# The causal mask moved from GpSimd to TensorE in a one-core attention + mixture-of-experts block, with its neighbours reordered

## The chip, the core and the metric

One NeuronCore of a Trainium2 chip runs the whole block as one program. The metric is the device time of that program in microseconds (us), the median of the runs shown. Lower is better. The five engines run side by side: TensorE (PE, with its weight loads as PEld), VectorE (DVE), ScalarE (ACT), GpSimd (POOL) and SyncE (SP, which here only issues transfers). They meet through semaphores: each engine works its own list in order and stops at a wait until the count is reached.

## What is computed

```python
x = L0_attn_x                                   # 4 sequences x 256 tokens x 512
xn = _layernorm(x)
# attention: 32 heads of 16, 8 key/value groups of 4 heads
scores = jnp.einsum('bhqd,bhkd->bhqk', q, k)
scores = jnp.where(causal, -jnp.inf, scores)    # key later than query
weights = softmax(scores * HD**-0.5)
att = (weights @ v) @ Wo + bo
# experts: 16, the 4 best of each token, plus one shared expert
z = silu(x @ Wg.T) * (x @ Wu.T)
ffn = sum_over_chosen(cw * (z @ Wd.T)) + shared
out = x + att + ffn
```

## The kernel before

The 1024 tokens are normalised first. An opening stretch (to about 124 us of the span) projects queries and keys, splits them into bf16 parts and stores them in HBM, runs the shared expert over eight tiles of 128 tokens (n = 0 to 7), and builds the routing tables. It writes x plus the shared expert's result to `out` in HBM.

Then comes the main stretch: **47 slots** of 128 routed token rows. In one, TensorE transposes the gathered rows of the next slot (`rows_transpose`, L1219), multiplies by the slot's expert in two halves (`gate_up_half` 0 and 1, L1178), transposes the gated result of the slot before (`z_transpose`, L1186), and does the down product of two slots back (`down`, L1168). The slot's expert may be a new one: then SP has loaded its weights (`load`, L364, one of two buffers) and told ACT so (`announce`, L360, a wait for the landing and then a count); ACT makes their high part (L635), DVE the low part of the gate and up weights (`gu_low`, L994) and POOL the low part of the down weights (`down_low`, L500). TensorE's `gate_up_half` 0 waits for DVE's.

Attention is threaded through the slots. Each of the four sequences b has twelve slots j and eight groups g of four heads; the table `BESIDE = ((0, 1), (2,), (3,), (4, 5), (6,), (7, 8), (9,), (10, 11))` says which slots lie beside which group. In a group's first slot TensorE makes the transposed scores of the group (`scores`, L1285 and L1287, keys on partitions, into banks 0 to 2), ACT takes their exponential (`numerators`, L707; the tile is `pexp`, which lies in `xn` and is called xn in the rows), and TensorE then puts other scores into the same three banks, from which DVE finds the maxima of the group four ahead (`scores_for_max`, L1198 and L1203; `maxima`, L979). The two calls share the banks, so each waits for the other's reader. The `numerators` are split into two fp16 parts, `phi` by ACT (`high16`, L713) and `plo` by DVE (`low16`, L1036), which TensorE multiplies with the values in the next group (`weighted`, L1301). Between `numerators` and `high16`, POOL sets to zero the entries whose key is later than the query (`causal`, L484, two selects per group).

The maxima of four groups are collected (`negm_split`), transposed by TensorE (`maxima_transpose`, L1210), copied by ACT and sent by ACT's queue into two extra rows of the query tile (`minus_maxima`, L666 and L668, semaphore `nm_in`). `scores` of groups 0 and 4 waits for that transfer.

POOL's list in a slot is: the group's selects, the gather of the slot three ahead (`gather`, L475), the indirect add of a finished slot into `out` (`add_rows`, L495, 256 KB, tile `ysb`), then `down_low`. All adds into `out` are strictly one after the other, since rows may repeat. Attention's result of a sequence (tile `att`, called xn in the rows) is added in one transfer of 512 KB (`add_attention`, L517), beside the next sequence's j = 4. ACT writes the `ysb` tile of a slot only when the add of two slots before has landed.

## Time and profile before

| | |
|---|---|
| median of 3 runs | 553.87 us (553.21 to 555.04) |
| the profiled execution | 553.7 us |
| its span in the trace | 552.0 us |
| mean granted TensorE clock | 0.945 |
| PE busy | 453.3 us |
| DVE busy | 357.0 us |
| ACT busy | 284.3 us |
| POOL busy | 274.6 us |

Busy time is the union of an engine's instructions over the span. The span leaves 1.7 us of the profiled execution outside. A timeline row gives start and length in us, counted from the span's start, and in brackets the idle time of that engine before the row and what ended it. The granted clock is the share of 2.4 GHz that TensorE had: 1.00 is 2.4 GHz and 0.50 is 1.2 GHz.

### The profile page before, as it was taken

What the parts mean: (1) busy time and instruction counts of PE and PEld (TensorE: products, weight loads), DVE (VectorE), ACT (ScalarE), POOL (GpSimd) and SP (SyncE); (2) the same over time, 40 slices, a digit from 0 to 9 for tenths busy, and PEclk for the clock granted to TensorE, in tenths of its full rate; (3) what the DMA queues carried; (4) which work ended last, traced back from release to release, by engine and by line L of the source; (5) the groups of instructions that cost most, each with busy time, mean ns of one, the idle gap of its engine ahead of it and who ended that gap; (6) DMA issues with size and microseconds to landing.
All of it is one profiled execution on the core that took longest, in us unless ns stands there. A gap on an engine that the chain in (4) does not pass through costs nothing.

```text
span 552.0 us, 9709 instructions
## 1 busy us (share of the span) xinstructions
PE 453.3 (82%) x2960; PEld 338.6 (61%) x2960; DVE 357.0 (65%) x604; ACT 284.3 (52%) x434; POOL 274.6 (50%) x235
## 2 busy tenths in 40 slices
PE   0998969968398899889987789987779999998870
PEld 0967748845276676557755567565556776766640
DVE  6488743776177678857779797578367655955620
ACT  2532222615266567745676577377276545756610
POOL 2111609632244575565467687263467534654630
PEclk9999979998699899999988899999979999998996
DMA  7915952549634644895588775856655433254233
GB/s 273 356 29 132 256 204 68 145 134 172 257 96 80 172 73 95 240 241 130 92 202 238 203 202 111 211 103 182 153 135 83 77 72 54 63 95 80 39 48 48
DMA packets 31813, 77.91 MB, mean 141 GB/s; under 512 B 3984, under 2 KB 11664, under 8 KB 28848
## 3 DMA queue, kind: packets, MB, share of 16 engines
q1 hardware_dynamic: 18864, 45.92, 27.1%
q0 software_dynamic: 11792, 27.27, 26.4%
q10 hardware_dynamic: 1104, 4.06, 3.5%
q8 instruction: 27, 0.44, 0.3%
q14 instruction: 26, 0.21, 0.1%
HBM read 54.04 MB, written 23.07 MB: 140 GB/s over the span
## 4 chain that ended last, share of the span: by engine, by line
PE 37%; DMA 24%; DVE 13%; ACT 8%; issue 8%; POOL 3%; SPq 2%; ACTq 1%; DVEq 1%; POOLq 0%
PE psum L1178 10%; DMA out<-ysb,tab 9%; PE psum L1168 8%; DMA wraw<-wexp 5%; DMA q_parts<-stage 3%; PE psum L1198 3%; PE psum L1313 3%; DVE wsplit L994 3%; ACT xn L707 3%; DMA out<-xn 3%; DVE plo L1036 3%; PE psum L1131 2%; ACT wsplit L635 2%; PE psum L1203 2%; PE psum L1115 2%
## 5 line engine op out<-in xcount | busy, mean ns | idle before, releaser
L1178 PE MATMUL psum<-wsplit,xgT 128*128 x564 | 163.2, 428 | 14.6 <-DVE wsplit L994 14.5
L495 POOL DMA_INDIRECT out<-ysb,tab x47 | 81.8, 1740 | 127.8 <-ACT ysb L660 87.0
L1178 PEld LDWEIGHTS psum<-wsplit,xgT 128*128 128x128 f32 x564 | 105.3, 200 | 35.2 <-issue 17.4
L1168 PE MATMUL psum<-wsplit,zT 128*128 (+1 forms) x330 | 87.7, 401 | 9.6 <-issue 4.6
L1036 DVE TENSOR_TENSOR plo<-xn,phi 128x1536 f16<-128x1536 f32 x32 | 63.4, 1980 | 36.7 <-ACT phi L713 35.2
L1168 PEld LDWEIGHTS psum<-wsplit,zT 128*128 128x128 f32 x330 | 61.0, 188 | 25.8 <-issue 13.4
L989 DVE TENSOR_TENSOR xgT<-psum,xgT 128x512 fp32r<-128x512 f32 x47 | 32.3, 687 | 53.5 <-ACT xgT L631 53.2
L475 POOL DMA_INDIRECT xg<-xn_rows,tab x47 | 57.1, 1215 | 17.3 <-PE psum L1219 8.8
L979 DVE TENSOR_REDUCE negm<-psum 128x4 f32<-128x512 f32 x64 | 58.6, 949 | 7.4 <-PE psum L1203 7.4
L484 POOL TENSOR_SCALAR_AFFINE_SELECT xn<-xn 128x512 f32<-128x512 f32 x64 | 53.3, 961 | 20.2 <-ACT xn L707 20.2
L635 ACT ACTIVATE wsplit<-wraw (+1 forms) x48 | 48.8, 1048 | 15.5 <-SPq L360 9.7
L707 ACT ACTIVATE xn<-psum 128x1536 f32<-128x1536 f32 x32 | 46.3, 1446 | 19.5 <-PE psum L1287 12.4
L500 POOL TENSOR_TENSOR wsplit<-wraw,wsplit (+1 forms) x16 | 45.4, 2838 | 20.6 <-ACT wsplit L635 20.4
L660 ACT ACTIVATE ysb<-psum,tab 128x512 f32<-128x512 f32 x47 | 32.2, 685 | 45.1 <-PE psum L1168 40.1
L713 ACT ACTIVATE phi<-xn 128x1536 f16<-128x1536 f32 x32 | 47.3, 1477 | 10.1 <-POOL xn L484 9.9
L625 ACT ACTIVATE wqk_sb<-psum 128x256 f32<-128x256 f32 x47 | 18.1, 384 | 54.5 <-PE psum L1186 54.1
L994 DVE TENSOR_TENSOR wsplit<-wraw,wsplit (+1 forms) x32 | 37.9, 1222 | 7.1 <-ACT wsplit L635 6.3
L1131 PE MATMUL psum<-xT,wqk_sb 128*128 128x256 f32 x128 | 31.5, 403 | 5.1 <-DVE stage L808 5.1
L612 ACT ACTIVATE th<-psum 128x256 f32<-128x256 f32 x55 | 20.8, 377 | 26.3 <-PE psum L1178 15.5
L1219 PE MATMUL psum<-ident,xg 128*128 128x128 f32 x188 | 29.7, 281 | 4.9 <-DMA xg<-xn_rows,tab 4.9
L1131 PEld LDWEIGHTS psum<-xT,wqk_sb 128*128 128x128 f32 x128 | 25.7, 203 | 10.3 <-DVE stage L808 5.5
L1313 PE MATMUL psum<-wo_sb,stage 128*128 128x512 f32 x64 | 28.8, 595 | 2.2 <-ACT stage L717 1.9
(185 smaller groups left out, 721.4 us busy)
## 6 DMA issues: line engine op xcount, KB each, us to landing
wraw<-wexp SPq DMA_DIRECT2D x17, 1024.0 KB, 6.4
wraw<-wexp SPq DMA_DIRECT2D x17, 512.0 KB, 4.1
q_parts<-stage SPq DMA_DIRECT2D x16, 192.0 KB
xn<-x SPq DMA_DIRECT2D x4, 512.0 KB, 5.5
xn_rows<-xn SPq DMA_DIRECT2D x8, 256.0 KB, 6.2
ctxs<-x SPq DMA_DIRECT2D x8, 256.0 KB, 4.5
out<-ysb SPq DMA_DIRECT2D x8, 256.0 KB, 3.0
out<-xn POOLq DMA_DIRECT2D x4, 512.0 KB, 5.9
```

The lines of the kernel that those rows point to most:

```text
L475: nc.gpsimd.indirect_dma_start(out=xg[:, par, :], out_offset=None, in_=xn_rows, in_offset=rows_of(s)).then_inc(xg_in[par], 16)
L484: nc.gpsimd.affine_select(out=block_, in_=block_, compare_op=ALU.is_ge, fill=0.0, base=0, pattern=[[0, REP], [1, P]], channel_multiplier=- ...
L495: nc.gpsimd.indirect_dma_start(out=out, out_offset=rows_of(s), in_=ysb[:, par, :], in_offset=None, compute_op=ALU.add).then_inc(y_out[par] ...
L635: S(wsplit[:, place, 0, cols], wraw[:, place, cols], ACT.Copy).then_inc(w_high[part], 1)
L707: S(pexp[:, g % 2, :], psum[:, 0:3, :].rearrange("p a n -> p (a n)"), ACT.Exp, scale=SCALE).then_inc(exp_done, 1)
L713: S(phi[:, g % 2, :], pexp[:, g % 2, :], ACT.Copy).then_inc(hi16_done, 1)
L979: V.tensor_reduce(negm[:, g // 4, 0, REP * (g % 4):REP * (g % 4) + REP, qt], s_, AX.X, ALU.max, negate=True).then_inc(negm_done, 1)
L994: V.tensor_tensor(wsplit[:, place, 1, HALVES[half]], wraw[:, place, HALVES[half]], wsplit[:, place, 0, HALVES[half]].bitcast(F32), ALU.sub ...
L1036: V.tensor_tensor(plo[:, g % 2, :], pexp[:, g % 2, :], phi[:, g % 2, :], ALU.subtract).then_inc(lo16_done, 1)
L1131: last = MM(psum[:, dst, i * T:(i + 1) * T], wqk_sb[:, k, f * P:(f + 1) * P], xT[:, k, T * b:T * (b + 1)], start=k == 0, stop=k == KD - 1, ...
L1168: last = MM(dst, lhs(a, k), split_weights(place, w, c), start=m == 0, stop=m == len(products) - 1)
L1178: last = MM(bank(GUB[par]), xgT[:, par, a, k, :], split_weights(place, w, k * 512), start=k == 0 and a == w == 0, stop=k == KD - 1 and a = ...
```

## The change

The select on POOL is taken out. After the score matmuls of a group, TensorE adds, in the same three banks, the product of `mask_b` (minus 1e30 above the diagonal) with the identity onto the diagonal blocks: two matmuls of 256 columns and one of 512. `high16` waits for the exponential alone.

Beside it:

- TensorE runs 18 transposes of the identity (`WARM`) once the last part of x has landed.
- SP announces expert 1 and loads expert 2 before it issues the six transfers that pack the second sequence's queries and keys (`pack_one`); three of these follow the load of expert 2, three that of expert 3, and the load of `wo` follows that of expert 5.
- Attention's sum is added in two transfers of 256 KB, the first beside j = 3, the second beside j = 4, each after the add of one slot.
- TensorE's `maxima_transpose` and ACT's `minus_maxima` move to the start of their slot.
- TensorE's `scores_for_max` moves from between the halves of `gate_up_half` to behind the second half.
- DVE's `gu_low` of the first expert moves: its two halves go behind `slot_gates` and behind the last `z_low` and the first `x_low` of the opening.

```diff
 # SP
+            announce(0, 1)
             ...
-            for i in range(6):
-                pack_one(sp, i, 1)
-            sp.wait_ge(table_ps, 2)
-            sp.dma_start(wo_sb[:, :, :], wo).then_inc(wo_in, 16)
-            announce(0, 1)
             for e in range(2, NE):
                 load(0, e)
+                if e in (2, 3):
+                    for i in range(3 * e - 6, 3 * e - 3):
+                        pack_one(sp, i, 1)
+                if e == 5:
+                    sp.wait_ge(table_ps, 2)
+                    sp.dma_start(wo_sb[:, :, :], wo).then_inc(wo_in, 16)
 # POOL
-                if s > SPS and s % SPS == 3:
-                    pool.wait_ge(att_out, 16 * (s // SPS) + 16)
+                if s > SPS and s % SPS in (2, 3):
+                    pool.wait_ge(att_out, 32 * (s // SPS) + (0 if s % SPS == 2 else 16))
             ...
-            def add_attention(b):
-                pool.wait_ge(att_sb, QT * b + (QT + 1))
-                newest = SPS * (b + 1) + 2 if b < B - 1 else NSLOT - 1
+            def add_attention(b, qt):
+                pool.wait_ge(att_sb, QT * b + qt + 2)
+                newest = SPS * (b + 1) + 1 + qt if b < B - 1 else NSLOT - 1
             ...
                 for g in range(G):
-                    causal(b, g)
             ...
-                        if b and j == 4:
-                            add_attention(b - 1)
+                        if b and j in (3, 4):
+                            add_attention(b - 1, j - 3)
 # ACT
             def high16(b, g):
-                act.wait_ge(masked, 2 * (G * b + g + 1))
+                act.wait_ge(exp_done, G * b + g + 2)
             ...
+                        if j == BESIDE[g][-1] and (g == 3 or g == 7 and not last):
+                            minus_maxima(2 * b + (g // 4 + 1), 1 - g // 4)
                         if s + 1 < NSLOT:
                             x_high(s + 1, 1 - par)
                         if s:
                             z_rows(s - 1)
-                        if j == BESIDE[g][-1] and (g == 3 or g == 7 and not last):
-                            minus_maxima(2 * b + (g // 4 + 1), 1 - g // 4)
 # DVE, the opening
                 if n == 6:
                     slot_experts()
-                    gu_low(0, 1, 0)
                 if n == 7:
                     slot_gates()
-                    gu_low(0, 1, 1)
+                    gu_low(0, 1, 0)
             z_low(NT - 1, 1, ZB)
             x_low(0, 0)
+            gu_low(0, 1, 1)
 # PE
+            pe.wait_ge(x_in[3], 16)
+            for i in range(WARM):
+                TR(bank(DN, P), ident[:, :], ident[:, :])
             ...
                 MM(psum[:, 2, :], k_packs[b % 2][rows, g, P:T], q_packs[b % 2][rows, h0:h0 + REP, P:T],
-                   start=True, stop=True).then_inc(st_ps, 1)
+                   start=True, stop=False, skip_group_check=True)
+                for pr in range(2):
+                    MM(psum[:, pr, :].rearrange("p (h t) -> p h t", h=2)[:, :, 0:P], mask_b[:, :],
+                       ident_b[:, :].rearrange("p (a n) -> p a n", a=1).broadcast_to([P, 2, P]),
+                       start=False, stop=True, skip_group_check=True)
+                MM(psum[:, 2, :].rearrange("p (h t) -> p h t", h=REP), mask_b[:, :],
+                   ident_b[:, :].rearrange("p (a n) -> p a n", a=1).broadcast_to([P, REP, P]),
+                   start=False, stop=True, skip_group_check=True).then_inc(st_ps, 1)
```

How the instructions stand. The first place is SP's list at the end of the opening, where `ysb` is the shared expert's result, `xT` and `wqk_sb` hold the packed queries and keys of the second sequence, and `wraw` receives expert weights (2048 columns are a gate and up part). Before:

```order
L352 DMA out<-ysb 128x512 x3
L287 DMA xT<-q_parts 48x8192
L290 DMA wqk_sb<-k_parts 48x1x2048
L287 DMA xT<-q_parts 32x1x8192
L290 DMA wqk_sb<-k_parts 32x1x2048
L287 DMA xT<-q_parts 16x8192
L290 DMA wqk_sb<-k_parts 16x2048
L373 DMA wo_sb<-wo 128x2048
L364 DMA wraw<-wexp 128x2048 x2
L364 DMA wraw<-wexp 128x1024
```

After:

```order
L353 DMA out<-ysb 128x512 x3
L365 DMA wraw<-wexp 128x2048
L288 DMA xT<-q_parts 48x8192
L291 DMA wqk_sb<-k_parts 48x1x2048
L288 DMA xT<-q_parts 32x1x8192
L365 DMA wraw<-wexp 128x2048
L291 DMA wqk_sb<-k_parts 32x1x2048
L288 DMA xT<-q_parts 16x8192
L291 DMA wqk_sb<-k_parts 16x2048
L365 DMA wraw<-wexp 128x1024
```

Expert 2's load stands ahead of all six pack transfers, expert 3's in the middle of them, and `wo` is gone from this place.

The second place is TensorE's list in the first slot of a group, from the scores of the group on (`q_pack` and `k_pack`; `ident,xg` is `rows_transpose`, `wsplit,xgT` is `gate_up_half`). Before, the scores and what follows them:

```order
L1285 MATMUL psum<-q_pack,k_pack 128x512 x2
L1287 MATMUL psum<-q_pack,k_pack 128x512
L1219 MATMUL psum<-ident,xg 128x128 x4
```

After:

```order
L1280 MATMUL psum<-q_pack,k_pack 128x512 x2
L1282 MATMUL psum<-q_pack,k_pack 128x512
L1285 MATMUL psum<-ident_b,mask_b 128x2x128 x2
L1288 MATMUL psum<-ident_b,mask_b 128x512
L1214 MATMUL psum<-ident,xg 128x128 x4
```

Three matmuls with the mask now stand between the scores and the transposes of the next slot's rows.

The third place is the middle of the same slot, where the matmuls with `ident_b` are those of `scores_for_max` and `ident,zz` is `z_transpose`. Before:

```order
L1178 MATMUL psum<-wsplit,xgT 128x512 x2
L1198 MATMUL psum<-k_pack,q_pack 128x128 x4
L1203 MATMUL psum<-mask_b,ident_b 128x512
L1198 MATMUL psum<-k_pack,q_pack 128x256 x4
L1203 MATMUL psum<-mask_b,ident_b 128x2x128 x2
L1186 MATMUL psum<-ident,zz 128x128 x2
L1178 ISA
L1178 MATMUL psum<-wsplit,xgT 128x512
```

After, from the last matmuls of the second half on:

```order
L1173 MATMUL psum<-wsplit,xgT 128x512 x2
L1193 MATMUL psum<-k_pack,q_pack 128x128 x4
L1198 MATMUL psum<-mask_b,ident_b 128x512
L1193 MATMUL psum<-k_pack,q_pack 128x256 x4
L1198 MATMUL psum<-mask_b,ident_b 128x2x128 x2
L1260 TENSOR_LOAD where
L1260 ISA x2
```

The scores for the maxima stood ahead of the z transposes and the second half; they now stand behind both, ahead of the reading of the next slot's expert and the down product.

## Rows read from the trace of the kernel before

**Rows 1.** The page, engines: busy us, share of the span, instructions.
```profile
PE 453.3 (82%) x2960; PEld 338.6 (61%) x2960; DVE 357.0 (65%) x604; ACT 284.3 (52%) x434; POOL 274.6 (50%) x235
```
**Rows 2.** Who waited for whom: us in total, times, longest.
```profile
PE psum L1198 <- ACT xn L707: 20.6, 15, 7.1
...
PE psum L1178 <- DVE wsplit L994: 14.5, 11, 2.9
...
ACT phi L713 <- POOL xn L484: 9.9, 3, 6.8
...
PE psum L1285 <- DMA xT<-negmT: 5.3, 4, 2.3
...
PE psum L1285 <- DMA q_pack<-negmT: 4.1, 2, 2.3
```
**Rows 3.** Timeline of PE, start of the opening.
```profile
14.16 1.94 PE L1106 MATMUL psum<-ident,xn 128*128 128x128 f32 x8 [14.16 <-DVE xn L790]
...
20.52 0.60 PE L1106 MATMUL psum<-ident,xn 128*128 128x128 f32 x4
...
21.94 0.60 PE L1106 MATMUL psum<-ident,xn 128*128 128x128 f32 x4
```
**Rows 4.** Timeline of PE, end of the opening.
```profile
121.26 1.79 PE L1168 MATMUL psum<-wsplit,zT 128*128 128x512 f32 x6 [2.28 <-DVE zT L965]
```
**Rows 5.** Timeline of ACT and PE, slots 1 and 2.
```profile
141.88 0.66 PE L1219 MATMUL psum<-ident,xg 128*128 128x128 f32 x4 [4.02 <-DMA xg<-xn_rows,tab]
...
147.27 1.06 ACT L635 ACTIVATE wsplit<-wraw  x1 [9.65 <-SPq L360]
...
149.72 0.61 PE L1198 MATMUL psum<-k_pack,q_pack 96*128 96x128 bf16 x4 [5.16 <-ACT xn L707]
```
**Rows 6.** The chain that ended last, there: start, us, what.
```profile
128.62 17.91 DMA wraw<-wexp
```
**Rows 7.** Timelines of PE, DVE and ACT, slots 3 and 4.
```profile
159.14 0.40 PE L1198 MATMUL psum<-k_pack,q_pack 96*128 96x128 bf16 x4 [0.40 <-ACT xn L707]
...
160.03 0.38 PE L1203 MATMUL psum<-mask_b,ident_b 128*128 128x256 bf16 x2
160.25 0.38 PE L1186 MATMUL psum<-ident,zz 128*128 128x128 f32 x2
...
161.85 1.54 PE L1168 MATMUL psum<-wsplit,zT 128*128 x6
...
166.89 0.40 PE L1198 MATMUL psum<-k_pack,q_pack 96*128 96x128 bf16 x4 [0.41 <-ACT xn L707]
...
160.21 1.81 DVE L979 TENSOR_REDUCE negm<-psum 128x4 f32<-128x512 f32 x2
...
163.43 0.69 ACT L660 ACTIVATE ysb<-psum,tab 128x512 f32<-128x512 f32 x1 [0.99 <-PE psum L1168]
...
165.39 1.45 ACT L707 ACTIVATE xn<-psum 128x1536 f32<-128x1536 f32 x1
```
**Rows 8.** The chain, third sequence and last: attention's add.
```profile
384.63 9.80 DMA out<-xn
...
486.63 5.75 DMA out<-xn
...
493.19 4.63 DMA out<-ysb,tab
```
**Rows 9.** Timelines of POOL and PE, slot 31.
```profile
395.24 1.63 POOL L495 DMA_INDIRECT out<-ysb,tab  x1 [7.91 <-DMA out<-xn]
...
404.28 0.61 PE L1198 MATMUL psum<-wqk_sb,xT 96*128 96x128 bf16 x4 [7.05 <-ACT xn L707]
```
**Rows 10.** Busy us by stretch, then clock, DMA share, GB/s.
```profile
143.00:153.30 10.30, 5.14 (x20) 3.47 (x20) 2.52 (x3) 3.65 (x5) 4.36 (x4) 0.50 0.51 179
...
385.40:388.80 3.40, 2.92 (x8) 2.02 (x9) 1.72 (x4) 2.15 (x3) 1.63 (x2) 0.50 0.86 161
402.50:409.30 6.80, 5.02 (x19) 3.91 (x20) 4.37 (x6) 4.42 (x7) 5.68 (x5) 0.50 0.68 161
```

More of the change, by code:

```diff
@@ L63 @@
 EARLY = 4
+WARM = 18
 MAXIMA_AT = {2: 0, 3: 1, 4: 2, 5: 3}
@@ L476, in gather @@
                                              in_offset=rows_of(s)).then_inc(xg_in[par], 16)
-            def causal(b, g):
-                pool.wait_ge(exp_done, G * b + g + 2)
-                first = pexp[:, g % 2, 0:1024].rearrange("p (r q) -> p r q", r=REP)[:, :, 0:P]
-                second = pexp[:, g % 2, 1024:1536].rearrange("p (r q) -> p r q", r=REP)
-                for block_ in (first, second):
-                    nc.gpsimd.affine_select(out=block_, in_=block_, compare_op=ALU.is_ge, fill=0.0, base=0,
-                                            pattern=[[0, REP], [1, P]], channel_multiplier=-1).then_inc(masked, 1)
             def add_rows(s):
@@ L551, in _ @@
                 sequence(b, b == B - 1)
-            pool.wait_ge(att_out, 16 * B + 16)
+            pool.wait_ge(att_out, 16 * QT * B + 16)
         @block.scalar
@@ L1334, in sequence @@
                             scores(b, g, G * b + (min(g + 4, G) if last else g + 4))
+                        if j == BESIDE[g][-1] and (g == 3 or g == 7 and not last):
+                            maxima_transpose(G * b + (g + 5), 1 - g // 4)
                         if s + 1 < NSLOT:
@@ L1350, in sequence @@
                             scores_for_max(b, G * b + (g + 4), (g + 4) % G)
-                        if j == BESIDE[g][-1] and (g == 3 or g == 7 and not last):
-                            maxima_transpose(G * b + (g + 5), 1 - g // 4)
-                        if s:
-                            pe.wait_ge(y_sb, s - 1)
-                            z_transpose(NT + s - 1, 1 - par, DN)
-                        if s < NSLOT:
-                            gate_up_half(par, place, 1)
                         if b and j == 0:
```

19 lines of the change are left out of this document (12 added, 7 removed).

## The prediction

> **What bounds the kernel now.** I read the engines' busy times first, then who waited for whom, then the chain that ended last, and then timelines of the places where TensorE stood still.
>
> TensorE is busy 82% of the span, DVE 65%, GpSimd 50% [rows 1]. So the change puts work on the fullest engine, and pays only if TensorE's idle time goes. TensorE's largest wait is that of `scores_for_max` for the exponential: 20.6 us in 15 waits [rows 2]. Two of them are large, 5.16 us in slot 2 [rows 5] and 7.05 us in slot 31 [rows 9]; the other 13 are 8.4 us together. DVE's low part of new weights holds TensorE 14.5 us in 11 waits, and the transfer of the maxima 9.4 us in 6 [rows 2].
>
> The two large waits have their causes elsewhere. In slot 2 ACT stood 9.65 us for SP [rows 5]: it wanted the announcement of expert 1's down weights, and in SP's list that stands behind the wait for expert 2's load, which took 17.91 us [rows 6] because six pack transfers and `wo` were issued ahead of it. In slot 31 the add of attention took 9.80 us [rows 8], POOL's next add waited 7.91 us for it [rows 9], the select stood behind that add, `phi` behind the select (its longest wait is 6.8 us [rows 2]), the exponential behind `phi`, and TensorE behind the exponential.
>
> The end is bound by something else: from attention's add at 486.63 on, each add into `out` is issued some 0.8 us after the landing of the one before (486.63 + 5.75, then 493.19) [rows 8]. TensorE has slack there.
>
> **The change, part by part.** The sum is made against the profiled execution, 553.7 us, which is 0.2 us below the median.
>
> *Mask matmuls.* Not in the trace in this place, but `scores_for_max` has the same ones: two of 256 columns take 160.25 - 160.03 = 0.22 us of TensorE's time [rows 7]. The change has these and one of 512, as many columns again: 0.44 us a group at 2.4 GHz. Of the 32 groups the last four lie in the end that the adds bound, so 28 x 0.44 = **+12.3**. Bounds: 28 x 0.22 = 6 if half hides in other waits, 18 if part of them runs at half clock.
>
> *`scores_for_max` behind the second half.* In a plain slot ACT's row goes: down product ends (161.85 + 1.54), `ysb` at 163.43, `phi`, exponential from 165.39 to 166.84 [rows 7]. So it is ready 3.5 us after the down product. TensorE does the weighted product, the scores, the transposes and half 0 in between and waits 0.4 us. Behind the z transposes and half 1 (161.85 - 160.25 = 1.60 us [rows 7]) it finds the exponential there. That takes the 13 short waits away: **-8.4**. (In a plain slot this and the mask cancel: -0.40 and +0.44.)
>
> The move has a price on DVE. `maxima` stands ahead of `z_rest`, `gu_low`, `gated` and `low16` in DVE's list, and DVE now stops at it. Its two reductions began at 160.21 [rows 7], just as the scores were ready; these now come 1.60 - 0.40 = 1.2 us later. Where the next slot has no new expert, DVE makes this up in its idle time. Where it has one, `gu_low` is late and half 0 of the next slot waits. 15 experts follow the first in 47 slots, 28 of which have maxima, so some 9 slots have both (15 x 28 / 47; eight, by the order of the weights in the timeline). In some DVE is late by its own work anyway and the effect may be anything from nothing to 1.6. I take 0.6 each: **+5**. Bounds: 0, and 8 x 1.6 = 13.
>
> *SP's order.* Expert 2's load goes out first, and the announcement that ACT stood for comes when expert 3's load and three packs are issued, before ACT gets there. The waits of 4.02 us (a gather landing late in that traffic) and 5.16 us [rows 5] go, and the half clock that followed: PE was busy 5.14 us at 0.50 in 143.0 to 153.3 [rows 10], which is 2.6 us more than at 1.00. Against that, slot 0's own `gu_low` for slot 1 comes behind the moved maxima, and I take 1.6 for it. 9.2 + 2.6 - 1.6: **-10**. If the gather stays late the 4.02 stay, so the bounds are -6 and -12. The load of `wo` moved behind expert 5's gate part delays only transfers that have several us to spare: 0, and 2 us if they had none.
>
> *Slot 31.* `phi` no longer waits for POOL, and POOL waits for half of attention's add at a time. 7.05 us [rows 9] go, and half of the 5.02 us at half clock behind it [rows 10], 2.5. The new weights of the next slot would then hold TensorE about 1.0. **-8.5**. Bounds: -5 (the down weights, which POOL makes behind the adds, take over the wait) and -10. What is late next is the add itself: `ysb` of slot s needs the add of s - 2, and with 4.6 us of landing for an add [rows 8] and two halves between, the adds still keep ahead of slots of 7.75 us (166.89 - 159.14 [rows 7]).
>
> *Maxima's transposes and transfers.* ACT sends the maxima some 2 us earlier, an estimate: they pass `x_high` and `z_rows`, which waits for TensorE's half 0 (1.6 us, as half 1), but `high16` of the slot before is still in front. Of 9.4 us [rows 2] some 1.1 lie in the end bound by adds, and I leave 1.8: **-6.5**. Bounds: -3, -8. The transpose now stands ahead of `rows_transpose`; if DVE's maxima are late, all of the slot waits for it.
>
> *Opening.* TensorE started at 14.16, and the fourth tile began at 20.52 where the pace is 21.94 - 20.52 = 1.42 us a tile [rows 3]: three tiles at full pace and the first copy's 1.0 us would be at 18.1 or so. 18 transposes ahead warm the engine in time it stood idle: **-2** (0, if the granted clock does not rise before 14 us or the stretch is regained in the HBM stores behind it). One half of DVE's `gu_low` stood ahead of the `z_low` for which TensorE waited 2.28 [rows 4]; I take half of that wait: **-1.1** (0 to -2).
>
> *Attention's sum in halves, at the end.* Whole, it took 5.75 and a gap of 0.8 in the serial chain [rows 8]. A half of 256 KB isn't in the trace: below it lies 2.9 (half of 5.75), above it 4.63 (a slot's indirect add, also 256 KB [rows 8]). I take 4.2, nearer to the indirect add, as both are mostly latency. Two of them with their gaps are 10.0 against 6.55, and I take half of these 3.4 as hidden, since the first half goes while POOL would wait for the next `ysb`: rounded, **+1.6**. Bounds: -1 and +4. 
>
> *Clock elsewhere.* Slot 30's half-clock stretch, 2.92 us busy [rows 10], follows waits that go: **-1.5** (0 to -8).
>
> Sum: +12.3 - 8.4 + 5 - 10 - 8.5 - 6.5 - 2 - 1.1 + 1.6 - 1.5 = -19.1. 553.7 - 19.1 = 534.6, with the 0.2 to the median **535 us**.
>
> **The rivals.**
>
> *Clean.* All half-clock stretches vanish. The mean clock of 0.945 is 2 x 0.055 x 552 = 61 us at half clock, up to 30 us of TensorE's time if it were the bound in all of them. I have counted 9 (2.6, 2.5, 1.5 and the opening's 2); of the other 21 a third is -7: 528 us. Against it: DVE's waits for new experts stay, and stretches at half clock follow them. The Trainium skill (TensorE: Matmul & The Clock Gate, What's actually happening) says that throttled is the default and activity releases it, which favours this rival; the trace agrees so far that every half-clock stretch I looked at lies behind a stall. Chance 0.15.
>
> *The waits move to DMA.* The gather, weights or down low parts take over in slots 2 and 31 (+4.0 and +3.5, the terms' bounds), the maxima arrive as late as before on some occasions (+2): 544 us. For it: transfers took 17.91 us in one crowd [rows 6] and 9.80 in another, against 5.75 [rows 8]. Chance 0.20.
>
> *DVE becomes the bound (slower).* If DVE has no idle time to make up the moved maxima, each of 28 groups costs 1.2 to 1.6 instead of eight at 0.6: 28 x 1.4 - 5 = +34, 569 us. It decides from the point where some 14 of the 20 plain groups lose 1.4. Against it: DVE is busy 65% [rows 1], so it has 0.35 x 7.75 = 2.7 us a slot, more than 1.4, and TensorE needs its gated result only behind the next slot's half 0. A part of it, in the crowded stretch from 285 to 330 us, is likelier. Chance of a time over 555: 0.05.
>
> *No pay.* The mask's 12 us and DVE's 5 eat stalls that were only hidden copies of others, and what is gained in slots 2 and 31 is given back before the end, where the adds bound: 553. Against it: the adds' chain starts when TensorE delivers slot 38. Chance 0.05.
>
> **How the numbers follow.** The forecast has 0.55, with a range of its own of 529 to 541. The range is **524 to 547**: below it lies half of the clean case and all bounds together, above it the two last cases. A change within 0.3% (1.7 us) can't be told from none. Faster: 0.55 + 0.15 + 0.20 = 0.90; same 0.04; slower 0.06.
>
> **What would show it.** TensorE's wait for the exponential falls from 20.6 to under 4 us; no 9 us wait of ACT on SP; slot 2's gate products start by 139; PE busy rises by about 12 us; the wait on DVE's weights rises from 14.5 to some 18; the wait on the maxima's transfer is 1 to 3 us; the first projection starts 2 us earlier. Halves land in 3 to 4.7 us. The prediction is wrong if DVE's `maxima` waits turn up as TensorE waits in plain slots, if the span between two first slots without a new expert is not 7.7 to 7.9 us, or if the adds are still issued back to back long before 480 us.

## The result and the profile after

The changed kernel takes **536.81 us** (median of 4 runs, 534.90 to 537.62) against 554.45 us of the kernel before on the same chip (4 runs, 553.21 to 555.67): a ratio of 0.968 (0.964 to 0.971). The numbers in brackets behind a ratio are its 95% interval. Timed a second time, beside experiments 9 to 11, the same two kernels took 536.71 us (6 runs, 531.8 to 542.1) and 551.23 (17 runs), 0.974 (0.968 to 0.981). The kernel before had medians of 550.7 to 554.5 us in the four timings of this document, so between kernels that weren't timed together I read no difference under 4 us. Medians take in every execution; the ratios leave out the few that ran in a slower state, over 1.5% above the fastest. The profiled execution took 536.95 us, its span 535.1 us, at a mean clock of 0.952.

The page after, the engines (busy us, share, instructions) and the chain that ended last:
```profile
PE 462.7 (86%) x3074; PEld 345.7 (65%) x3074; DVE 361.4 (68%) x604; ACT 283.4 (53%) x434; POOL 235.5 (44%) x175
...
PE 48%; DMA 17%; DVE 15%; issue 7%; ACT 5%; SPq 2%; ACTq 1%; POOL 1%; DVEq 1%; POOLq 0%
```
TensorE has 9.4 us more work than in [rows 1] and GpSimd 39 less. TensorE is half of the chain in this execution. In a profile of another execution of the same kernel (experiment 12) it is 30% and the transfers 31%, so this share says little about the kernel.

Who waited for whom after (total, times, longest; L1193 is `scores_for_max`, L1173 the gate product, L1214 `rows_transpose`, L1280 the scores, L971 DVE's maxima, L627 ACT's high parts of weights, L1205 `maxima_transpose`, L977 DVE's split of the maxima into parts):
```profile
PE psum L1173 <- DVE wsplit L986: 17.7, 12, 3.4
...
PE psum L1214 <- DMA xg<-xn_rows,tab: 8.3, 5, 4.0
...
PE psum L1205 <- DVE negm L977: 2.0, 1, 2.0
...
PE psum L1280 <- DMA xT<-negmT: 0.4, 1, 0.4
...
PE psum L1193 <- ACT xn L699: 0.2, 1, 0.2
...
DVE negm L971 <- PE psum L1198: 25.1, 21, 4.8
...
ACT wsplit L627 <- SPq L361: 1.3, 1, 1.3
```
Against [rows 2] the exponential's 20.6 us are 0.2 and the maxima's transfer 9.4 are 0.4 (2.0 in the profile of experiment 12). The moved `maxima_transpose` has a wait of its own, 2.0 us for DVE in slot 23, which the kernel before didn't have. What is left are DVE's new weights (14.5, now 17.7) and the gathers. DVE waits 25 us for `scores_for_max`, but TensorE has no wait for DVE in a plain slot.

To see where the time goes between those places I read the start of `rows_transpose` in nine slots from each trace of TensorE (us from the span's start; the last column is the span). The same table serves the experiments. Each row is one profiled execution, and such a one lay up to 5 us from its kernel's median (below it in `e6` and `e7`, above it in `e10`):
```
slot             0     3    11    12    20    24    31    33    42   end
before       125.1 156.8 216.7 226.5 295.7 333.2 395.1 416.9 487.6 552.0
after        121.5 144.9 201.5 211.9 279.6 321.8 382.3 402.1 473.4 535.1
e1_select    121.2 144.2 199.1 207.5 281.2 322.1 383.9 404.6 473.7 539.6
e2_sfm_mid   123.3 148.1 206.0 220.9 290.9 329.9 390.1 411.2 482.4 544.0
e3_sp_old    122.1 152.6 209.2 219.6 287.9 329.4 391.9 412.3 483.6 545.8
e4_whole     122.1 145.5 202.1 210.9 281.9 320.9 383.6 402.9 474.1 534.8
e5_mask_al.  124.7 156.7 215.0 225.0 292.4 328.1 389.6 406.7 478.8 539.6
e6_maxtr_old 123.2 146.5 204.7 220.0 290.4 329.2 390.6 405.1 477.0 538.2
e7_opening   125.2 147.6 204.3 213.0 284.4 322.8 383.6 400.2 471.4 533.8
e8_split     121.1 143.8 199.8 208.1 278.6 317.1 380.5 397.8 468.4 530.6
e9_no_mask   121.5 145.3 200.2 208.6 278.2 319.1 379.7 398.9 468.0 530.9
e10_sel.+mid 120.5 147.8 205.8 219.5 292.0 330.5 393.6 416.0 486.8 552.4
e11_spl.+wh. 122.8 145.7 201.7 209.9 276.8 317.1 380.1 397.4 468.2 528.5
```
The lead is 3.6 us at slot 0, 11.9 at slot 3, 14.6 at slot 12, 16.1 at slot 20, then 11.4 at slot 24, 14.8 at slot 33 and 16.9 at the end. So it is won by slot 12 for the most part, and some of it is handed back in slots 20 to 23.

**Opening.** Timeline of PE; before, the fourth tile's transposes began at 20.52 [rows 3]:
```profile
13.29 1.12 PE L1101 MATMUL psum<-ident,xn 128*128 128x128 f32 x8
...
17.20 0.60 PE L1101 MATMUL psum<-ident,xn 128*128 128x128 f32 x4
```
The first eight take 1.12 us where they took 1.94 [rows 3], and the fourth tile begins 3.3 us earlier.

**Slots 1 to 3.** Timeline of PE, its one long wait of this stretch, and of ACT where it had waited 9.65 us [rows 5]; then busy us by stretch, clock and DMA share, as in [rows 10]:
```profile
130.50 2.92 PE L1173 MATMUL psum<-wsplit,xgT 128*128 x6 [3.42 <-DVE wsplit L986]
...
137.22 1.06 ACT L627 ACTIVATE wsplit<-wraw  x1 [0.51 <-issue]
```
```profile
127.00:137.00 10.00, 6.58 (x20) 4.62 (x20) 7.09 (x9) 3.79 (x7) 0.95 (x1) 0.66 0.96 193
137.00:145.00 8.00, 8.00 (x70) 6.06 (x68) 4.70 (x10) 5.58 (x8) 4.01 (x3) 1.00 0.68 179
```
Neither the gather's 4.02 us nor the exponential's 5.16 is left. A wait of 3.42 us for DVE's weights in slot 1 remains (1.90 before), with half clock around it (0.66 in the first stretch). Slot 2 runs at full clock.

**Slots 31 and 32.** Timelines of PE, POOL and DVE, and a pair of the same DVE instructions elsewhere (457.08):
```profile
390.82 0.66 PE L1214 MATMUL psum<-ident,xg 128*128 128x128 f32 x4 [1.80 <-DMA xg<-xn_rows,tab]
394.50 2.92 PE L1173 MATMUL psum<-wsplit,xgT 128*128 x6 [3.03 <-DVE wsplit L986]
...
382.43 1.61 POOL L488 DMA_INDIRECT out<-ysb,tab  x1 [5.60 <-DMA out<-xn]
...
389.15 2.93 POOL L493 TENSOR_TENSOR wsplit<-wraw,wsplit  x1
...
388.53 5.77 DVE L986 TENSOR_TENSOR wsplit<-wraw,wsplit  x2
...
457.08 2.35 DVE L986 TENSOR_TENSOR wsplit<-wraw,wsplit  x2
```
TensorE's 7.05 us wait of slot 31 [rows 9] is gone, but POOL still waits 5.60 us for attention's add; it only holds up a gather now, and not `phi`. In slot 32 the gather and DVE's weights take back 4.8 us. The two slots together went from 21.8 to 19.8 us (20.2 in the profile of experiment 12): 2 us, where I had counted 8.5.

**End.** The adds are back to back from 479 us on (the chain: start, us, what), before from 487 [rows 8]. The last row is of the eight halves of attention's sum, 256 KB each.
```profile
479.14 4.40 DMA out<-ysb,tab
```
```profile
DMA to landing us min/median/max: 4.0/4.4/7.1
```

### The profile page after: what moved, and what is told of

It reads as the page before. It is cut to its first block, busy times and chain, and to the rows that moved or that the text cites. A ratio compares the mean times of both kernels' runs of the same rounds, so it can differ in the third digit from the quotient of the medians.

```text
span 535.1 us, 9881 instructions
## 1 busy us (share of the span) xinstructions
PE 462.7 (86%) x3074; PEld 345.7 (65%) x3074; DVE 361.4 (68%) x604; ACT 283.4 (53%) x434; POOL 235.5 (44%) x175
## 4 chain that ended last, share of the span: by engine, by line
PE 48%; DMA 17%; DVE 15%; issue 7%; ACT 5%; SPq 2%; ACTq 1%; POOL 1%; DVEq 1%; POOLq 0%
PE psum L1173 17%; PE psum L1163 9%; DMA out<-ysb,tab 9%; DVE wsplit L986 6%; DMA q_parts<-stage 4%; PE psum L1315 3%; PE psum L1193 2%; PE psum L1126 2%; DVE plo L1028 2%; PE psum L1214 2%; PE psum L1303 2%; PE psum L1198 2%; PE psum L1181 2%; ACT wsplit L627 1%; PE psum L1280 1%
## 5 line engine op out<-in xcount | busy, mean ns | idle before, releaser
L1173 PE MATMUL psum<-wsplit,xgT 128*128 x564 | 163.0, 429 | 17.7 <-DVE wsplit L986 17.7
L1173 PEld LDWEIGHTS psum<-wsplit,xgT 128*128 128x128 f32 x564 | 106.3, 202 | 38.7 <-issue 20.6
L1163 PE MATMUL psum<-wsplit,zT 128*128 (+1 forms) x330 | 90.3, 409 | 7.6 <-DVE zT L957 3.5
L971 DVE TENSOR_REDUCE negm<-psum 128x4 f32<-128x512 f32 x64 | 59.6, 954 | 25.1 <-PE psum L1198 25.1
L478 POOL DMA_INDIRECT xg<-xn_rows,tab x47 | 62.9, 1338 | 29.5 <-PE psum L1214 14.3
L1163 PEld LDWEIGHTS psum<-wsplit,zT 128*128 128x128 f32 x330 | 59.3, 189 | 23.5 <-issue 12.5
L1028 DVE TENSOR_TENSOR plo<-xn,phi 128x1536 f16<-128x1536 f32 x32 | 59.1, 1847 | 15.0 <-ACT phi L705 12.9
L699 ACT ACTIVATE xn<-psum 128x1536 f32<-128x1536 f32 x32 | 46.3, 1446 | 23.0 <-PE psum L1288 14.8
L493 POOL TENSOR_TENSOR wsplit<-wraw,wsplit (+1 forms) x16 | 47.4, 2960 | 12.8 <-ACT wsplit L627 12.5
L627 ACT ACTIVATE wsplit<-wraw (+1 forms) x48 | 48.8, 1047 | 1.8 <-SPq L361 1.3
L986 DVE TENSOR_TENSOR wsplit<-wraw,wsplit (+1 forms) x32 | 42.4, 1364 | 1.0 <-ACT wsplit L627 0.8
L1214 PE MATMUL psum<-ident,xg 128*128 128x128 f32 x188 | 29.5, 281 | 8.3 <-DMA xg<-xn_rows,tab 8.3
L623 ACT ACTIVATE xgT<-psum 128x512 fp32r<-128x512 f32 x47 | 27.9, 594 | 11.0 <-issue 6.9
L1126 PEld LDWEIGHTS psum<-xT,wqk_sb 128*128 128x128 f32 x128 | 25.4, 201 | 10.7 <-DVE stage L800 6.0
L1214 PEld LDWEIGHTS psum<-ident,xg 128*128 128x128 f32 x188 | 23.0, 144 | 12.6 <-DMA xg<-xn_rows,tab 9.7
```

Source lines behind the costliest of these rows:

```text
L478: nc.gpsimd.indirect_dma_start(out=xg[:, par, :], out_offset=None, in_=xn_rows, in_offset=rows_of(s)).then_inc(xg_in[par], 16)
L493: nc.gpsimd.tensor_tensor(wsplit[:, place, 1, PARTS[1]], wraw[:, place, PARTS[1]], wsplit[:, place, 0, PARTS[1]].bitcast(F32), ALU.subtrac ...
L627: S(wsplit[:, place, 0, cols], wraw[:, place, cols], ACT.Copy).then_inc(w_high[part], 1)
L971: V.tensor_reduce(negm[:, g // 4, 0, REP * (g % 4):REP * (g % 4) + REP, qt], s_, AX.X, ALU.max, negate=True).then_inc(negm_done, 1)
L986: V.tensor_tensor(wsplit[:, place, 1, HALVES[half]], wraw[:, place, HALVES[half]], wsplit[:, place, 0, HALVES[half]].bitcast(F32), ALU.sub ...
L1028: V.tensor_tensor(plo[:, g % 2, :], pexp[:, g % 2, :], phi[:, g % 2, :], ALU.subtract).then_inc(lo16_done, 1)
```

## The experiments

Most are the changed kernel with one thing taken back; `e5_mask_alone` is the kernel before with one thing added, and `e8_split` and `e11_split_whole` go a step beyond the change. Ratios are to the kernel before, timed beside each. Code cuts are shortened: `...` stands for what is left out, and calls for their bodies. The runs of `e1`, `e2`, `e3`, `e5`, `e9`, `e10`, `e11` and of the changed kernel itself (0.974) are from one chip, `e4`, `e6`, `e7`, `e8` from another.

**1. The select back on GpSimd (`e1_select`).** ACT's `phi` waits for the select, TensorE adds nothing to the scores:
```
+def causal(b, g):  # two affine_select on pexp, then masked += 2
...
-    act.wait_ge(exp_done, G * b + g + 2)
+    act.wait_ge(masked, 2 * (G * b + g + 1))
...
-    for pr in range(2): MM(psum[:, pr, ...], mask_b, ident_b ...)
-    MM(psum[:, 2, ...], mask_b, ident_b ...)
```

> The changed kernel with the mask back as GpSimd's select; all reorderings stay. My prediction puts 12.3 us on the mask matmuls and takes the 6.8 us wait of phi on the select in slot 31 for most of that slot's loss. Theory A (the mask itself pays little, the reorderings pay): TensorE gets 28 x 0.44 = 12 us back, the select stands behind GpSimd's adds again and ACT waits for it some 10 us; with halves of attention's add the waits are shorter than in the kernel before. Time 530 to 540 us. Theory B (the mask on TensorE is what pays): phi, exponential and TensorE wait for the select in each crowded slot, 10 us or more above the changed kernel's 536.8, so 545 or more.

Measured: 541.21 us (537.9 to 544.4), 0.981 (0.976 to 0.986), between the bands of the two theories. Its waits:
```profile
ACT phi L716 <- POOL xn L487: 23.5, 7, 8.5
PE psum L1184 <- DVE wsplit L997: 22.4, 12, 4.4
...
PE psum L1204 <- ACT xn L710: 9.4, 3, 5.6
```
Plain slots are 7.2 us without the mask matmuls and 7.65 with them (`rows_transpose` of slots 3 and 4, `e1_select` and, from 144.88 on, after):
```profile
144.18 0.60 PE L1225 MATMUL psum<-ident,xg 128*128 128x128 f32 x4
...
151.39 0.60 PE L1225 MATMUL psum<-ident,xg 128*128 128x128 f32 x4
```
```profile
144.88 0.60 PE L1214 MATMUL psum<-ident,xg 128*128 128x128 f32 x4
...
152.52 0.60 PE L1214 MATMUL psum<-ident,xg 128*128 128x128 f32 x4
```
So the mask costs 0.44 us in such a slot as reckoned, and the select costs more than that in the fuller slots, where it stands in POOL's queue behind adds: the kernel with the select leads by 2.4 us at slot 11 and is 4.5 behind at the end.

**2. `scores_for_max` back between the two halves (`e2_sfm_mid`).**
```
 gate_up_half(par, place, 0)
+scores_for_max(...)
 z_transpose(NT + s - 1, 1 - par, DN); gate_up_half(par, place, 1)
-scores_for_max(...)
```

> The changed kernel with scores_for_max back between the two halves of the gate product. By my sum the move was worth -8.4 (13 short waits for the exponential) and +5 (DVE's low parts late), so undoing it gives 536.8 + 3.4 = 540 us, with TensorE's wait for the exponential back at 8 us or more and DVE's wait at its maxima (25.1 us now) back near the 7.4 of before. Rival: the 25.1 us that DVE now waits at the maxima is what fills TensorE's 17.7 us of waits for DVE's weights; then undoing it makes it faster, 530 us or less. A third: with the mask matmuls ahead of it, the exponential is 0.44 later still and the waits are 28 x 0.8 = 22 us, 550 us or more.

Measured: 543.99 us (540.2 to 545.7), 0.984 (0.978 to 0.989). DVE's weights hold TensorE less, which is the price of the move that I had feared, and the exponential and the maxima's transfer hold it more:
```profile
PE psum L1173 <- DVE wsplit L986: 10.7, 6, 4.0
...
PE psum L1280 <- DMA xT<-negmT: 7.5, 2, 6.2
PE psum L1193 <- ACT xn L699: 6.2, 6, 1.6
```
The price is real (17.7 against 10.7 us of waits), but the place between the halves costs more: the exponential holds TensorE 6.2 us, where I had set 8 or more, and `xT` 7.5, which I hadn't foreseen. Half of the loss falls in slot 11, which lasts 14.9 us here and 10.4 after; the last section shows what is late there.

**3. SP's old order (`e3_sp_old`).** Six pack transfers and `wo` ahead of the announcement of expert 1 and of expert 2's load:
```
-announce(0, 1)
 ...
+for i in range(6): pack_one(sp, i, 1)
+sp.wait_ge(table_ps, 2); sp.dma_start(wo_sb, wo)
+announce(0, 1)
 for e in range(2, NE):
     load(0, e)
-    ...            # the packs behind e = 2 and 3, wo behind e = 5
```

> The changed kernel with SP's order as before: six packs and wo ahead of expert 2's load, and the announcement of expert 1 behind them. By my sum this is worth 10 us: 547 us, with ACT waiting 9 us or more for SP in slot 1 and TensorE standing about as long in slot 2. Rival: slots 0 to 2 shrank because of the moved scores and the removed select, and SP's order is worth 3 us or less: 540.

Measured: 546.51 us (543.0 to 547.6), 0.988 (0.983 to 0.994). ACT's wait is back, TensorE's behind it, and the load ahead in the chain:
```profile
144.23 1.06 ACT L625 ACTIVATE wsplit<-wraw  x1 [6.87 <-SPq L361]
...
146.68 0.61 PE L1191 MATMUL psum<-k_pack,q_pack 96*128 96x128 bf16 x4 [5.21 <-ACT xn L697]
```
```profile
126.91 16.57 DMA wraw<-wexp
```
Slot 3 begins 7.7 us later than after, and the delay stays to the end (median +9.7; by the ratios 8 to 11). This is the term that came out most cleanly.

**4. The mask alone in the kernel before (`e5_mask_alone`).** The select and `masked` out, the mask matmuls in, and every order, transfer and the opening as before.

> The kernel before with nothing changed but the mask: TensorE's three matmuls in place of the select. By my sum: +12.3 for the matmuls at full clock (up to 14 with the slower ones), and in slot 31 about -8 since phi no longer waits for GpSimd: 554.5 + 4 = 558 us. With scores_for_max still between the halves each exponential is 0.44 us later where ACT isn't the one that is late, at most 2 us more in all: 560. Rival (GpSimd and its SBUF port were a hidden brake): the time falls below 550 us.

Measured: 544.44 us (540.8 to 549.9, 12 runs), 0.988 (0.983 to 0.992). I had the sign wrong. Plain slots last 7.74 us (156.71 to 164.45), as before the change, with the mask's 0.44 us in them:
```profile
156.71 0.60 PE L1208 MATMUL psum<-ident,xg 128*128 128x128 f32 x4
...
164.45 0.60 PE L1208 MATMUL psum<-ident,xg 128*128 128x128 f32 x4
```
TensorE's wait for the exponential was 20.6 us [rows 2] and is:
```profile
PE psum L1187 <- ACT xn L696: 10.2, 5, 6.4
```
In the old order a loop through ACT sets the slot: down product, `ysb`, `phi`, exponential (3.5 us [rows 7]), then `scores_for_max`, half 1 and the next down product. The mask matmuls lie beside ACT's part, in the 0.40 us for which TensorE waited, and cost nothing in these slots. What the select held up in the fuller slots is gone too: slots 31 and 32 last 17.1 us, against 21.8.

**5. Attention's sum whole (`e4_whole`).** One add of 512 KB for each sequence in place of two of 256 KB, at POOL's old place, with the matching waits.

> The changed kernel with attention's sum in one transfer of 512 KB again. By my sum the halves cost 1.6 us at the end and help slot 31 by about 3: so 536.8 + 1 = 538 us. If the adds bound the end alone (a fixed cost for each transfer decides), whole is faster: 535. If slots 31 and 32 depend on it (the down weights that GpSimd makes behind the adds), 541 or more.

Measured: 534.93 us (528.2 to 540.9), 0.967 (0.959 to 0.975): 1.9 us less than the changed kernel, within what runs differ. Halving brings nothing that can be measured. At the median a half lands in 4.4 us and the whole in 6.0:
```profile
out<-xn POOLq DMA_DIRECT2D x4, 512.0 KB, 6.0
```

**6. Maxima's transposes and transfer at their old place (`e6_maxtr_old`).**
```
 gate_up_half(par, place, 0)
+maxima_transpose(...)      # PE: was ahead of rows_transpose
 x_high, z_rows
+minus_maxima(...)          # ACT: was ahead of these
```

> The changed kernel with the transposes and transfer of the maxima back at their old place, ahead of the z transposes and ACT's high parts of weights. By my sum the move is worth 6.5 us: 543 us, with TensorE's wait on the transfer of the maxima back at 7 to 9 us. Rival: in the changed kernel the slot is longer anyway (the maxima's scores stand at its end), and the transfer's wait would be the same or larger since DVE's maxima are later: 545 or more. Second rival: worth nothing, 537, since weights of new experts hold those slots.

Measured: 545.23 us (539.1 to 550.1, 12 runs), 0.988 (0.984 to 0.993). The wait that the edit was to remove is back, the longest of it in slot 11:
```profile
217.87 1.01 PE L1280 MATMUL psum<-xT,wqk_sb 98*128 98x512 bf16 x2 [5.07 <-DMA xT<-negmT]
```
```profile
PE psum L1280 <- DMA xT<-negmT: 8.7, 4, 5.1
```
With the transfers into `q_pack` it is 12.3 us, more than the 9.4 of the kernel before. The profiled execution is a short one (span 538.2, at the lower end of its runs). In it slot 12 is 8.1 us late, and 5 of them come back in slots 31 and 32, where this kernel has no large wait.

**7. Opening as before (`e7_opening_old`).** The 18 transposes of the identity are left out, `gu_low` of the first slot is in its old place. The two parts were not undone apart.

> The changed kernel without the 18 warming transposes and with DVE's low part of the first expert at its old place. By my sum 2.0 + 1.1 = 3.1 us: 540 us, with TensorE's rows of the first slot 3.5 us later than in the changed kernel. Rival: the end is bound by a chain that does not start in the opening: 537.

Measured: 540.10 us (535.5 to 541.8), 0.982 (0.977 to 0.988). Slot 0 begins 3.7 us later. Its profiled execution, again at the lower end, has 1.1 of these left at slot 12, and none at slot 33; the medians differ by 3.3, within what two timings differ by.

**8. The wait for the low weights split (`e8_split`).** Half 0 of the gate product waits only for the first half of the low part:
```
+pe.sem_inc(w_low[0], 1)                       # once, so that no wait is on zero
-sp.wait_ge(w_low[part], (2 - part) * (e - 1))
+sp.wait_ge(w_low[part], (2 - part) * (e - 1) + (1 - part))
+pe.wait_ge(w_low[0], 2 * number + 1)          # ahead of half 1
```
Half 0 keeps its wait for `2 * number`, which one part less now reaches, because the count starts at one.

> The changed kernel, but TensorE's first half of the gate product waits only for the first half of the weights' low part and the second half waits for the second (in the changed kernel the first half waits for both). Theory: TensorE's 17.7 us of waits for DVE's weights in 12 places are real waits on the path; each shrinks by the 1.2 us of one DVE subtraction, the second half comes 1.6 us later and finds its part: 12 x 1.2 = 14 us less wait, of which the places bound by DVE itself give little: 527 to 531 us. Rival: DVE is the bound in those slots, and what is saved in one place is waited for in the next: 535 or more.

Measured: 533.30 us (532.3 to 535.2), 0.971 (0.966 to 0.976).
```profile
PE psum L1215 <- DMA xg<-xn_rows,tab: 14.6, 6, 4.5
...
PE psum L1174 <- DVE wsplit L986: 6.7, 5, 2.2
```
11.0 us of waits on DVE go and 6.3 us of waits for gathers come: the waits move from one cause to the next, and the difference of 4.7 is near the 4.5 us that the span is shorter. That the time falls isn't shown by this run alone: 0.971 stands against 0.968 and 0.974 of the changed kernel.

**9. No mask at all (`e9_no_mask`).** The changed kernel without the mask matmuls and without a select. It leaves the causal mask out and so computes another function; it only prices the mask.

> The changed kernel without the mask matmuls and without GpSimd's select: it leaves the causal mask out altogether, so every query attends to later keys too. It prices the mask on TensorE. Theory 1 (the plain slots are bound by TensorE after the change, spacing 7.65 us against 7.21 in the run with the select): 28 groups by 0.44 us is 12 us less than the changed kernel, about 525 us, with plain slots 7.2 us apart. Rival (the mask lies in time in which TensorE would wait anyway, as it did in the order of before): not over 4 us less, 533 us or more, with plain slots at 7.5 us or more.

Measured: 530.80 us (530.1 to 535.2), 0.967 (0.962 to 0.972), 5.9 us under the changed kernel timed beside it (4 by the ratios) and between the two theories. Plain slots are 7.2 us, as theory 1 says:
```profile
145.30 0.60 PE L1214 MATMUL psum<-ident,xg 128*128 128x128 f32 x4
...
152.49 0.60 PE L1214 MATMUL psum<-ident,xg 128*128 128x128 f32 x4
```
```profile
PE psum L1173 <- DVE wsplit L986: 19.8, 13, 3.4
PE psum L1214 <- DMA xg<-xn_rows,tab: 13.4, 9, 4.5
```
But the waits for weights and gathers rise by 2.1 and 5.1 us, more than half of what the mask gives back. The lead is 3.3 us at slot 12 and 1.4 at slot 20. TensorE has 10.0 to 13.5 us less work (449.2 us busy against 459.2 and 462.7 in two profiles of the changed kernel) for 4 to 5.9 us of time, so a microsecond saved on TensorE is worth about half a microsecond or less here.

**10. Both back (`e10_select_mid`).** Experiments 1 and 2 together.

> The changed kernel with the select back on GpSimd and with scores_for_max back between the two halves of the probabilities' work: the fourth corner beside the changed kernel, the select alone back (0.981) and the move alone back (0.984). Theory 1 (ScalarE's loop of eviction, phi, exp and the maxima sets the old order's slot of 7.75 us, whoever does the mask, and the select adds its own waits only in the fuller slots): both losses add up, 0.995 of before less the mask's hidden part, about 548 us, with exp waits of 15 us or more on TensorE. Rival (the two edits only pay together, each one back costs the same seven us as both): 0.982, about 541 us.

Measured: 549.80 us (546.3 to 555.1, 12 runs), 0.998 (0.995 to 1.002). Of the four corners, select and old place is 549.8, mask and old place 544.0, select and new place 541.2, mask and new place 536.7. The mask is worth 5.8 us at the old place and 4.5 at the new one, the move 8.6 and 7.3. By the ratios they are 8 and 4, 10 and 5. So each is worth something with the other in place and without it. The medians fit a plain sum, but the intervals leave some 5 us of interplay open. In plain slots there is interplay: with the select they last 7.74 us at the old place and 7.21 at the new, with the mask matmuls 7.75 and 7.64, so the matmuls cost time only at the new one.

It also says that everything else of the change together (SP's order, opening, maxima, halves) is worth nothing measurable as long as these two are as before. The same holds with the mask matmuls in: experiment 2 has all the rest and took 543.99 us, experiment 4 has none of it and took 544.44 beside it. So it is the old place of `scores_for_max` that hides the rest, whoever does the mask. The move alone in the kernel before was not run. The profile, of an execution 4 us above its median, shows where the lead goes. Slot 3 begins at 147.8, 9.0 us ahead of before; the lead is 7.0 at slot 12, 3.7 at slot 20, 1.5 at slot 31. In slot 31 (POOL, ACT and PE, and the chain's start, us, what):
```profile
394.02 1.62 POOL L498 DMA_INDIRECT out<-ysb,tab  x1 [8.07 <-DMA out<-xn]
...
397.38 1.81 POOL L487 TENSOR_SCALAR_AFFINE_SELECT xn<-xn 128x512 f32<-128x512 f32 x2
...
399.22 1.48 ACT L716 ACTIVATE phi<-xn 128x1536 f16<-128x1536 f32 x1 [9.35 <-POOL xn L487]
...
403.04 0.61 PE L1204 MATMUL psum<-wqk_sb,xT 96*128 96x128 bf16 x4 [7.35 <-ACT xn L710]
```
```profile
383.64 9.56 DMA out<-xn
```
The row of the prediction's first part (add, POOL, select, `phi`, exponential, `scores_for_max`) is here in full, with attention's sum in halves: halving doesn't always shorten it. The half that is issued here took 9.56 us for 256 KB, where the whole took 9.80 for 512 KB [rows 8].

**11. Split wait and whole sum (`e11_split_whole`).** Experiments 8 and 5 together.

> The changed kernel with the wait for the low weights split (each half of the gate product waits for its own half of the low part, which gave 0.971 of before in another call at 533.3 us) and the attention's sum transferred whole again. Theory 1 (the split takes 10 us of waits on VectorE away, of which 4 us reach the end, and the gathers' waits that it uncovered, 14.6 us, come from GpSimd being held at the adds of the halves; the whole transfer frees it): about 529 us, gather waits on TensorE under 10 us. Rival (the gathers are late through the ring of transfers itself, not through GpSimd's queue): no gain over the split alone, 533 us or more, gather waits stay at 14 us.

Measured: 530.39 us (526.5 to 535.3), 0.964 (0.958 to 0.970), against 536.7 and 0.974 of the changed kernel timed beside it. It is the fastest of all that computed the whole function.
```profile
PE psum L1174 <- DVE wsplit L986: 12.3, 8, 2.6
...
PE psum L1215 <- DMA xg<-xn_rows,tab: 6.1, 4, 4.2
```
The gathers' waits fall from 14.6 to 6.1 us with the whole sum, as theory 1 has it, and the weights' rise from 6.7 to 12.3. Their sum is 18.4 against 21.3 us. Whether the whole sum adds to the split (533.3 in another timing) is within the spread and stays open. That the two together beat the change is shown beside it, by little more than the intervals.

**12. The changed kernel again (`c_after`).**

> The changed kernel itself, unchanged, on the same chip as the three others of this call, so that they have a common base. Ratio to the kernel before 0.968 (0.964 to 0.972), about 536 us; if the ratio lies outside 0.960 to 0.975, the differences between calls are larger than the effects that I read from them.

Measured: 536.71 us and 0.974, as above. The ratio lies at the edge of the band that I had set, the median within 0.1 us of the first.

## Why the prediction was right, point by point

The total (535 us) was right within 2 us, and that is in part luck: too large and too small terms cancelled, and the terms don't add up in the way that the sum supposed.

*Mask, +12.3.* The working was right where it says that a slot holds 0.44 us more. As a term of the sum it was too large. Alone it costs nothing in plain slots (experiment 4), and in the changed kernel taking it out gives 5.9, or 4 by the ratios (experiment 9). PE's busy time rose by 9.4 us (5.9 in the profile of experiment 12) and not by 12.3, though without the mask it is 10.0 to 13.5 less (449.2 in experiment 9). The rest of TensorE's work became 4 us shorter than the 453.3 of [rows 1], at a mean clock of 0.957 there where it was 0.945.

*The select's going.* I gave it a term only in slot 31. The runs show some 10 us for the select alone (541.2 in experiment 1, 530.8 in experiment 9; 8 by the ratios), 4.5 to 5.8 net of the mask matmuls, spread over the slots where the select stood behind an add. This term is missing in the sum: of three waits of `phi` (9.9 us [rows 2]) I used only the largest.

*The move, -8.4 + 5.* Both mechanisms work as forecast. The exponential's wait fell to 0.2 us, and DVE's weights hold TensorE 7.0 us more with the move than without (experiment 2), near the 5. The net is -7.3 to -8.6 (-5 to -10 by the ratios), not -3.4; the rest lies in waits that only the old place has when the transfers are late, in slot 11 above all. Those the prediction didn't have.

*SP's order, -10.* Measured 9.7 (experiment 3). The gather's wait went, as the central value supposed. The wait for DVE's weights in slot 1 grew by 1.5 us (1.90 to 3.42), where I had set 1.6. The half clock didn't go, as the 2.6 of this term supposed, but moved (0.66 in 127 to 137 us). For `wo` at its new place I had set 0, "2 us if they had none" to spare. In the changed kernel it costs nothing visible, but in experiments 2, 6 and 10 the wait behind it is 5 to 6 us.

*Slot 31, -8.5.* Slots 31 and 32 gave 2.0. The "new weights of the next slot", to which I gave 1.0, take 3.03, and the gather 1.80. What the sum has too much here it has too little in the select's term above.

*Maxima, -6.5.* The wait went from 9.4 to 0.4 or 2.0, and 2.0 came at the moved transpose, against which I had warned. Taking the edit back costs 8.4 by the medians, 3.1 in the profiled execution, and in it lies the delay in slot 11, which isn't what the term was made of. The sign is right, and the size isn't settled.

*Opening, -3.1.* Slot 0 began 3.6 us earlier; taken back, 3.3, within the noise.

*Halves, +1.6.* A half landed in 4.4 us at the median, where I had taken 4.2, and in up to 7.1. Taking them back gave 1.9, with the right sign and within the noise. The Trainium skill (DMA: Bandwidth & Descriptors, Anatomy of one DMA) puts the fixed part of a transfer at about 2.0 us; here it would be 2 x 4.4 - 6.0 = 2.8, an estimate from the two medians. The direction agrees, the size is larger for these adds.

*Clock elsewhere, -1.5.* The half-clock stretch of slot 30 is still there in the profile after (3.4 us from 368.1 on) and gone in that of experiment 12. All such stretches together were 61 us of the span and are 51 and 41. The rival "clean" supposed that they vanish, and they didn't.

*Sum of single steps.* Mask and move together give 13.1 (experiment 10 to the changed kernel), SP's order 9.7, maxima 8.4, opening 3.3: 34 us, and the whole change gave 14.5 to 17.6. Each was measured with all others in place. With mask and move out, the rest gives nothing. So the terms aren't independent, which the sum supposed: a late start hides in later waits, and an early start is eaten by them. The rival "no pay" describes just this, and is true of the half-made change, not of the whole. Of "the waits move to DMA" a part is true as well: the waits for gathers rose from 4.9 to 8.3 us.

*What would show it.* It held that exp waits are under 4, ACT's wait on SP gone, slot 2's gate product by 139 (137.6), projection 2 us earlier (it was 3.3), the median half in 3 to 4.7, DVE's weights at 18 (17.7), and adds back to back only from 479. PE's busy time rose by less than 12. The maxima's wait was 0.4 in one profile and 2.0 in the other, where I had set 1 to 3. Plain slots are 7.65, under the 7.7 to 7.9 outside which I had called the prediction wrong: I had the move at -0.40 in such a slot, and it gives -0.53 (7.74 to 7.21), against 0.43 for the mask.

## What to carry to other kernels

Ask of each plain stretch which loop closes it. Work laid beside another engine's part of that loop is free (the mask beside ACT: 0 of 12 us), and its price appears only when the loop is opened (0.44 us a slot). Test edits in pairs as well as alone: three edits that cost 3 to 10 us each when taken back gave nothing together as long as a fourth, the place of `scores_for_max`, was undone. An undo can also cost what the edit never gave, when it pushes a small transfer behind large ones. A wait that goes in one slot often comes back in the next through another cause, so read the lead over the kernel before at several places, not only at the place of the edit.

## What was not expected of the hardware

- Two of DVE's `TENSOR_TENSOR` (L986, both inputs in SBUF) took 5.77 us in slot 32 beside one of POOL's `TENSOR_TENSOR` of 2.93 us, and 2.35 elsewhere. 2.35 + 2.93 = 5.28: DVE stood still for as long as POOL took, and some more. The Trainium skill (SBUF — State Buffer, SBUF: two separate sides) says of such a pair that the one which starts first has the shared port for its whole instruction and the other waits. The trace agrees on the length of the wait (4.64 us for the one, 1.22 at the median), but not on who goes first: DVE's pair is recorded 0.62 us ahead of POOL's (388.53, 389.15). And at 115 us two of them overlap by 0.7 us and neither is longer than elsewhere. Before the change none of the 32 took over 1.30 us, so an order can bring such a meeting. It isn't what sets slots 31 and 32: the profile of experiment 12 has no such meeting there, and the two slots last 20.2 us.
- In slot 11 a transfer of 16 KB, the packed maxima into `xT`, holds TensorE 5.07, 5.80 and 6.18 us in experiments 6, 10 and 2, where `scores_for_max` or the maxima's transposes are back at their old place. It holds it not at all there in the changed kernel, and 2.3 at the most in the kernel before [rows 2], where both are old. The traces show what differs. SP issues `wo` (1 MB) and a gate and up part (1 MB) at this point, since the change put `wo` behind expert 5. In the changed kernel the maxima go out just ahead of them:
```profile
203.23 1.05 ACTq L660 DMA_DIRECT2D xT<-negmT  x1
...
204.34 0.43 SPq L379 DMA_DIRECT2D wo_sb<-wo  x1
```
  In experiment 2 they go out just behind, and TensorE goes on 11.0 us after the issue:
```profile
207.65 0.43 SPq L379 DMA_DIRECT2D wo_sb<-wo  x1
...
207.89 1.05 ACTq L660 DMA_DIRECT2D xT<-negmT  x1
...
218.86 1.01 PE L1280 MATMUL psum<-xT,wqk_sb 98*128 98x512 bf16 x2 [6.18 <-DMA xT<-negmT]
```
  By the landings in the traces, this transfer took 2.2 to 4.0 us in the eleven in which it goes out ahead of `wo`, or `wo` was loaded long before, and 7.1, 10.4 and 10.7 us in the three in which it goes out behind (experiments 6, 10 and 2). So SP's order and the other two edits are tied together through this one meeting: the change is 0.7 to 1.1 us on the good side of it. With `wo` elsewhere and one of the other edits undone nothing was run, so how much of the 7 and 8 us that these undos cost is this meeting stays open.
- Add transfers of 256 KB landed in 4.4 us at the median and of 512 KB in 6.0, but the longest of each trace took much more: 6.2 to 10.2 us for a half in the ten traces with halves, 8.9 to 10.5 for the whole in the four others.
